# The third phase's mask added by a product on TensorE, and a head's three maxima by one VectorE reduction

## The chip, the cores and the metric

The kernel runs on one core of a Trainium2 chip. The metric is device time in microseconds, the median over several executions. One further execution was recorded by the profiler, and all rows below come from that one.

## The reference

A two-layer decoder on a batch of 8 samples, 256 tokens, width 128: a linear attention (phase 0), a cross attention of 16 heads over 512 context tokens with a key mask (phase 1), a mixture of eight experts, a windowed causal attention of 16 heads (phase 2), a differential cross attention of 8 heads with a feed-forward network, and a last feed-forward network with ternary weights. The change touches phase 2 alone:

```python
def _L1_attn_ref(x, w_in, b_in, w_out, b_out):        # B=8, s=256, E=128
    B, S, E, H, W = (4, 256, 128, 16, 128)
    HD = E // H                                       # 8
    ...
    scores = jnp.einsum('bhqd,bhkd->bhqk', q, k) / jnp.sqrt(jnp.asarray(HD, x.dtype))
    i = jnp.arange(s)[:, None]
    j = jnp.arange(s)[None, :]
    allowed = (j <= i) & (j >= i - W)                 # causal, window of 128
    scores = jnp.where(allowed[None, None], scores, jnp.asarray(-1000000000.0, x.dtype))
    attn = jax.nn.softmax(scores, axis=-1)
```

The softmax needs, for each query and head, a maximum over the allowed keys.

## The kernel before, in words

Each of the 8 samples goes through five chains of steps (`to0` to `to3`, `end`), on three lanes, and through four attention cores, one for each phase. A core has two parts. In the **maxima** part, TensorE multiplies queries with keys, with the queries on the partitions, into one of two PSUM banks `mb`; VectorE takes each row's maximum into `mx`. After a group of four heads, GpSimd (POOL) splits the negated maxima into three bf16 parts `nm` (L798 to L802), TensorE turns them (L973), VectorE copies them to `mrow` (L1446), and a DMA puts them as extra rows beside the queries in `QP`. In the **exponentials** part, TensorE computes the scores again with the keys on the partitions and the maximum already subtracted, adding the mask by a product with the identity `identb` (L1012 in phase 1, L1007 in phase 2), into two banks `eb`; ScalarE takes the exponential (L1183), and TensorE multiplies with the values (L1042). A planner at the top of the file writes one fixed order for each engine from a table of estimated durations. TensorE's order interleaves the maxima of one core with the exponentials of another and with the chains' steps, and so does VectorE's. Each engine works strictly through its own order, so an instruction that waits holds all behind it.

A unit of maxima in phase 2 is one head. There are 8 samples x 16 heads = 128 units, in 32 groups of four. The unit waits until VectorE has finished with the unit two before (`max_used`, since `mb` has two banks). Then TensorE multiplies the first 128 queries with the first 128 keys (L981, 128 columns), and the second 128 queries with all 256 keys (L982, 256 columns). VectorE adds the mask and takes the maximum in one instruction for each product (L1454 and L1455): the custom instruction `tensor_tensor_reduce` adds `winq_add` (0 or -1e30 for three blocks of 128 x 128), writes the sum to `junk` and the maximum to `mx`. In the trace each of these is a CUSTOM_DVE_ANT_0 row and a DVE_READ_ACCUMULATOR2_ANT row. The second one increments `max_used`, which frees the bank for TensorE and, at a group's fourth unit, lets POOL begin on `nm`. Phase 1's units add their mask in the same way (L1451); phase 3's have no mask and use a plain `tensor_reduce` (L1459).

Of the kernel before, what the change touches and what calls it, by code (L numbers as in the profile page):

```python
# [11 lines left out]
ALU = mybir.AluOpType  # L12
ACT = mybir.ActivationFunctionType
AX = mybir.AxisListType

P = 128
B, S, D, SK = 8, 256, 128, 512
TQ, TK = S // P, SK // P
# [10 lines left out]
NEG_EXP = -3.0e38  # L29
# [10 lines left out]
MAX_UNITS = (0, 8, 4, 8)  # L40
# [10 lines left out]
LANES, SLOTS, WIDES, OUTS, OB, QN, MROWS = 3, 3, 2, 3, 1, 3, 4  # L51
# [330 lines left out]
def decoder(nc, x, ctxT, maskq, maskk, weights, columns, rows_in, experts_bias, out):  # L382
    with ExitStack() as ctx:
        def sb(name, shape, dt=F32):
            return ctx.enter_context(nc.sbuf_tensor(name, shape, dt))
# [10 lines left out]
        def sbs(n, name, shape, dt=F32):  # L396
            return [sb(f"{name}{i}", shape, dt) for i in range(n)]
# [6 lines left out]
        identb = sb("identb", [P, P], BF16)  # L404
# [5 lines left out]
        winq_add = sb("winq_add", [P, 3, P], BF16)  # L410
# [14 lines left out]
        V = sbs(SLOTS, "V", [P, TK, 16, VW])  # L425
        KV = sbs(SLOTS, "KV", [P, 16, VW])
        qf = sbs(SLOTS, "qf", [P, P])
        mx = sbs(SLOTS, "mx", [P, TQ, 16])
        nmr = sbs(SLOTS, "nmr", [P, TQ, 16])
        nm = sbs(SLOTS, "nm", [P, TQ, 16, PARTS], BF16)  # L430
        mrow = sbs(MROWS, "mrow", [MAX_ROWS, S], BF16)
# [22 lines left out]
        junk = sb("junk", [P, 2, SK], BF16)  # L454
# [54 lines left out]
        def q_of(core, h, n=1):  # L509
            return QW[core.wide][0:WIDE_ROWS, h:h + n] if core.p == 3 else QP[core.slot][:, h:h + n]  # L510

        def k_of(core, h, lo, n):
            return KS[core.slot][0:WIDE_ROWS, h, lo:lo + n] if core.p == 3 else KS[core.slot][:, h // 2, lo:lo + n]
# [4 lines left out]
        def wait_alone(eng):  # L518
            eng.nop(nofuse=True)
# [7 lines left out]
        class Chain:  # L527
# [5 lines left out]
            def done(self, ins):  # L533
                self.n += 1
                ins.then_inc(self.sem, 1)
# [4 lines left out]
            def link(self, ins, plain=False):  # L540
                self.done(ins)
                self.wait()
                if plain:
                    wait_alone(self.eng)
# [116 lines left out]
        def _(pool):  # L661
            chain = Chain(pool, pool_step)
            link, done = chain.link, chain.done
# [125 lines left out]
            def max_event(e):  # L789

                if e.kind != "max" or e.i != MAX_UNITS[e.core.p] - 1:
                    return
                slot, g = e.core.slot, e.g
                pool.wait_ge(max_used, e.n + 3)
                m = mx[slot][:, :, 4 * g:4 * g + 4]
                r = nmr[slot][:, :, 4 * g:4 * g + 4]
                n = [nm[slot][:, :, 4 * g:4 * g + 4, a] for a in range(PARTS)]
                done(G.tensor_scalar(n[0], m, -1.0, None, ALU.mult))  # L798
                link(G.tensor_scalar(r, m, -1.0, None, ALU.mult))
                link(G.tensor_tensor(r, r, n[0], ALU.subtract))  # L800
                link(G.tensor_copy(n[1], r))
                G.tensor_tensor(n[2], r, n[1], ALU.subtract).then_inc(nm_ready, 1)  # L802

            def values():

                for i in range(SLOTS):
                    yield 0.5 + 5 * i
                    link(G.memset(V[i][:], 0.0))
                    G.memset(V[i][:, :, :, 16:17], 1.0).then_inc(values_init, 1)

            program(max_event, nothing, chain_steps, values())

        @block.tensor
        def _(pe):
# [150 lines left out]
            def max_event(e):  # L965
                core, g, i = e.core, e.g, e.i
                pe.wait_ge(max_used, e.n + 1)
                bank = mb[:, e.n % 2, :]
                if e.kind == "turn":
                    pe.wait_ge(nm_ready, NM_N[core.p, core.b, g] + 1)  # L970
                    dst = bank.bitcast(BF16)
                    for t in range(TQ):
                        ins = nc.tensor.transpose(dst[0:MAX_ROWS, t * P:(t + 1) * P],  # L973
                                                  nm[core.slot][:, t, 4 * g:4 * g + 4, :].rearrange("p h c -> p (h c)"), identb[:])
                    ins.then_inc(max_scores, 1)
                    return
                if g == 0 and i == 0:
                    pe.wait_ge(stack_in[core.slot], IN_SLOT[core.p, core.b][2])
                if core.p == 2:
                    h = 4 * g + i  # L980
                    nc.tensor.matmul(bank[:, 0:P], q_of(core, h)[:, 0, 0:P], k_of(core, h, 0, P), start=True, stop=True)  # L981
                    ins = nc.tensor.matmul(bank[:, P:3 * P], q_of(core, h)[:, 0, P:2 * P], k_of(core, h, 0, S), start=True, stop=True)  # L982
                else:
                    h, t = 4 * g + i // 2, i % 2
                    ins = nc.tensor.matmul(bank, q_of(core, h)[:, 0, t * P:(t + 1) * P], k_of(core, h, 0, SK), start=True, stop=True)  # L985
                ins.then_inc(max_scores, 1)
# [73 lines left out]
            def prelude():  # L1060
# [4 lines left out]
                pe.wait_ge(masks_ready, 1)  # L1065

            program(max_event, exp_event, chain_steps, prelude())

        @block.scalar
# [134 lines left out]
        def _(dve):  # L1204
            chain = Chain(dve, dve_step)
            link, done = chain.link, chain.done
            V_ = nc.vector
# [229 lines left out]
            def max_event(e):  # L1437
                core, g, i = e.core, e.g, e.i
                slot = core.slot
                bank = mb[:, e.n % 2, :]  # L1440
                dve.wait_ge(max_scores, e.n + 1)
                if e.kind == "turn":
                    n = TURN_N[core.p, core.b, g]
                    if n >= MROWS:
                        dve.wait_ge(mrow_in[n % MROWS], MROW_TO[n - MROWS])
                    V_.tensor_copy(mrow[n % MROWS][:], bank.bitcast(BF16)[0:MAX_ROWS, 0:S]).then_inc(max_used, 1)  # L1446
                    return
                wait_alone(dve)
                if core.p == 1:
                    h, t = 4 * g + i // 2, i % 2  # L1450
                    ins = V_.tensor_tensor_reduce(junk[:, e.n % 2, :], bank, maskq_add[:, t, :], 1.0, NEG_EXP, ALU.add, ALU.max, mx[slot][:, t, h:h + 1])  # L1451
                elif core.p == 2:
                    h = 4 * g + i
                    V_.tensor_tensor_reduce(junk[:, e.n % 2, 0:P], bank[:, 0:P], winq_add[:, 0, :], 1.0, NEG_EXP, ALU.add, ALU.max, mx[slot][:, 0, h:h + 1])  # L1454
                    ins = V_.tensor_tensor_reduce(junk[:, e.n % 2, P:3 * P], bank[:, P:3 * P], winq_add[:, 1:3, :].rearrange("p a k -> p (a k)"), 1.0, NEG_EXP,  # L1455
                                                  ALU.add, ALU.max, mx[slot][:, 1, h:h + 1])
                else:
                    h, t = 4 * g + i // 2, i % 2
                    ins = V_.tensor_reduce(mx[slot][:, t, h:h + 1], bank, AX.X, ALU.max)  # L1459
                ins.then_inc(max_used, 1)  # L1460

            def exp_event(e):
# [4 lines left out]
                if u >= PROBS:  # L1467
                    dve.wait_ge(av_done, u - PROBS + 1)
                V_.tensor_tensor(probs[:, u % PROBS, :].rearrange("p (j q) -> p j q", j=4), eb[:, u % 2, :].rearrange("p (j q) -> p j q", j=4),  # L1469
                                 tri[:].unsqueeze(1).to_broadcast([P, 4, P]), ALU.mult).then_inc(probs_by[0], 1)  # L1470

            program(max_event, exp_event, chain_steps, prelude())


# [66 lines left out]
```

## Time and profile before

| | us |
|---|---|
| median of 3 executions | 1154.66 |
| lowest and highest | 1147.33, 1155.74 |
| the profiled execution, its own time | 1146.01 |
| its span in the trace | 1144.3 |
| mean granted TensorE clock over it | 0.906 of 2.4 GHz |

The span is from the first instruction's start to the last one's end. TensorE (PE) is busy in 75% of it, VectorE (DVE) in 58%, ScalarE (ACT) in 40%, GpSimd (POOL) in 33%. PEld is TensorE's weight load, which runs beside its products. "The chain of waits" follows the work that ended last back to its beginning, at each step to what released it; "issue" in it is time for which the profile shows no wait. Ends of TensorE's rows are modelled and overlap; the distance from one start to the next is what a row holds the engine for.

### The profile page before, as it was taken

To read this page: it belongs to the slowest core of one execution; us is meant where nothing else is said; L and a number is where in the kernel's file an instruction comes from. 1 tells how busy PE (TensorE), PEld (TensorE's weight loads), DVE (VectorE), ACT (ScalarE), POOL (GpSimd) and SP (SyncE) were. 2 spreads that over 40 slices of the span, in tenths; PEclk is the share of its full clock that TensorE was granted. 3 is DMA by queue.
4 is the path that set the end of the run, shared out by engine and by line. 5 is a ranking of instruction groups with operands and counts; after the bars stand their busy time and mean duration, and the time that the engine had idled before them with its cause. 6 is when DMAs were issued, how large, how long until landed. Compare 5 with 4: busy or idle time off the path is not lost.

```text
span 1144.3 us, 19524 instructions
## 1 busy us (share of the span) xinstructions
PE 854.7 (75%) x6459; PEld 481.8 (42%) x6522; DVE 667.8 (58%) x2234; ACT 459.3 (40%) x923; POOL 383.1 (33%) x872
## 2 busy tenths in 40 slices
PE   0466757988888887887787677888988777874666
PEld 0244544334333343444443455553534434651345
DVE  6646655667776764765677474376566484444431
ACT  0322213554444443544454222654645334651432
POOL 7524343210313222443223246433232125360033
PEclk9778978999999998999999888899999698995877
DMA  5357774031220204641233334543120602224100
GB/s 177 101 88 165 166 168 90 11 56 32 42 49 16 51 19 86 125 96 53 57 56 81 59 78 108 138 73 58 35 53 16 104 2 53 64 64 76 16 1 10
DMA packets 124964, 79.84 MB, mean 70 GB/s; under 512 B 8312, under 2 KB 122176, under 8 KB 124736
## 3 DMA queue, kind: packets, MB, share of 16 engines
q1 hardware_dynamic: 124864, 78.59, 33.2%
q8 instruction: 52, 0.85, 0.3%
q14 instruction: 48, 0.39, 0.1%
HBM read 43.99 MB, written 32.90 MB: 67 GB/s over the span
## 4 chain that ended last, share of the span: by engine, by line
PE 42%; DVE 21%; issue 10%; POOL 10%; DMA 8%; SPq 4%; ACT 4%; another core or an unknown queue 1%; DVEq 0%; POOLq 0%; ACTq 0%
PE ob L1042 7%; PE mb L985 5%; POOL hn L707 4%; DMA KS<-bounce 4%; DVE junk L1451 3%; PE side L861 3%; PE eb L1012 3%; PE eb L1013 2%; DVE mx L1459 2%; DMA QW<-bounce 2%; PE side L916 2%; DVE An L1391 2%; PE side L899 2%; PE side L908 2%; POOL rstd L695 2%
## 5 line engine op out<-in xcount | busy, mean ns | idle before, releaser
L1183 ACT ACTIVATE probs<-eb 128x512 f32<-128x512 f32 (+1 forms) x512 | 287.5, 571 | 401.9 <-PE eb L1013 172.7
L1451 DVE CUSTOM_DVE_ANT_0 junk<-mb,maskq_add 128x512 bf16<-128x512 f32 x256 | 172.1, 690 | 110.1 <-PE mb L985 82.3
L798 POOL TENSOR_SCALAR nm<-mx 128x8 bf16<-128x8 f32 x80 | 20.7, 259 | 428.7 <-DVE mx L1451 193.4
L1042 PE MATMUL ob<-probs,V 128*32 128x256 f32 (+1 forms) x2048 | 138.3, 390 | 3.3 <-ACT probs L1183 2.1
L1459 DVE TENSOR_REDUCE mx<-mb 128x1 f32<-128x512 f32 x128 | 85.0, 687 | 75.8 <-PE mb L985 74.0
L1012 PE MATMUL eb<-maskk_add,identb 128*128 128x512 bf16 x256 | 99.9, 390 | 6.6 <-DMA QP<-mrow 2.7
L985 PE MATMUL mb<-KS,QP 128*128 128x512 bf16 x230 | 89.0, 394 | 13.0 <-DVE mx L1451 12.1
L1013 PE MATMUL eb<-QP,KS 128*128 128x512 bf16 x233 | 90.6, 389 | 0.0
L1042 PEld LDWEIGHTS ob<-probs,V 128*32 128x32 f32 x2048 | 55.4, 113 | 77.7 <-issue 46.3
L985 PE MATMUL mb<-KS,QW 112*128 112x512 bf16 x128 | 53.0, 432 | 36.0 <-DMA QW<-bounce 21.3
L1454 DVE CUSTOM_DVE_ANT_0 junk<-mb,winq_add 128x128 bf16<-128x128 f32 x128 | 37.1, 290 | 68.1 <-PE mb L982 66.4
L707 POOL TENSOR_SCALAR hn<-X,mv,rstd 128x128 f32<-128x128 f32 x80 | 72.2, 910 | 4.3
L821 PE MATMUL side<-ident,hn 128*128 128x128 f32 x80 | 18.8, 322 | 64.0 <-POOL hn L707 62.6
L1190 ACT COPY OT<-ob 128x512 f32<-128x512 f32 x56 | 32.7, 584 | 73.0 <-PE ob L1036 52.2
L1469 DVE TENSOR_TENSOR probs<-eb,tri 128x512 f32<-128x512 f32 x64 | 42.3, 685 | 32.8 <-PE eb L1002 31.4
L713 POOL TENSOR_TENSOR xs<-xs,scratch 128x256 f32<-128x256 f32 (+1 forms) x32 | 30.4, 950 | 92.5 <-ACT scratch L1118 57.0
L861 PE MATMUL side<-ident,OT 128*128 128x36 f32 (+1 forms) x448 | 55.7, 281 | 5.6 <-issue 5.3
L861 PEld LDWEIGHTS side<-ident,OT 128*128 128x128 f32 x448 | 55.6, 198 | 9.9 <-issue 8.3
L1016 PE MATMUL eb<-QW,KS 112*128 112x256 bf16 x256 | 50.3, 292 | 9.8 <-ACT probs L1183 3.4
L701 POOL TENSOR_SCALAR rstd<-mv 128x2 f32<-128x2 f32 x64 | 16.0, 250 | 120.1 <-DVE mv L1247 118.3
L985 PEld LDWEIGHTS mb<-KS,QP 128*128 128x128 bf16 x256 | 25.7, 101 | 68.4 <-DVE mx L1451 40.1
L1455 DVE CUSTOM_DVE_ANT_0 junk<-mb,winq_add 128x256 bf16<-128x256 f32 x128 | 53.8, 420 | 0.2 <-issue 0.2
(186 smaller groups left out, 1706.0 us busy)
## 6 DMA issues: line engine op xcount, KB each, us to landing
QP<-bounce SPq DMA_DIRECT2D x48, 256.0 KB, 5.6
KS<-bounce SPq DMA_DIRECT2D x32, 384.0 KB, 7.5
bounce<-scratch SPq DMA_DIRECT2D x48, 192.0 KB, 2.3
bounce<-scratch SPq DMA_DIRECT2D x64, 128.0 KB, 2.1
KS<-bounce SPq DMA_DIRECT2D x32, 192.0 KB, 5.9
bounce<-scratch SPq DMA_DIRECT2D x16, 384.0 KB, 2.6
cT<-ctxT_dram SPq DMA_DIRECT2D x16, 256.0 KB, 2.9
bounce<-scratch SPq DMA_DIRECT2D x16, 256.0 KB, 3.0
```

The lines of the kernel that those rows point to most:

```text
L707: ins = G.tensor_scalar(dst[:, t, :], src[:, t, :], mv[l][:, t, 0:1], rstd[l][:, t:t + 1], ALU.subtract, ALU.mult)
L861: ins = nc.tensor.matmul(bank[:, lo:lo + 4 * n].rearrange("p (h e) -> p h e", e=n), OT[o][:, g, t * P:(t + 1) * P], chosen, start=True, st ...
L985: ins = nc.tensor.matmul(bank, q_of(core, h)[:, 0, t * P:(t + 1) * P], k_of(core, h, 0, SK), start=True, stop=True)
L1012: nc.tensor.matmul(part, identb[:], maskk_add[:, kt:kt + 1, :].to_broadcast([P, 2, S]), start=True, stop=False, skip_group_check=True)
L1013: ins = nc.tensor.matmul(part, k_of(core, h, kt * P, P), q_of(core, h, 2), start=False, stop=True, skip_group_check=True)
L1016: ins = nc.tensor.matmul(bank[:, j * S:(j + 1) * S], k_of(core, h + j, kt * P, P), q_of(core, h + j)[:, 0, :], start=True, stop=True)
L1042: ins = nc.tensor.matmul(bank[32 * j:32 * j + 32, S - n:S], v_of(core, kt, 4 * g + j), pr[:, (j % 2) * n:(j % 2 + 1) * n], start=(kt == 0) ...
L1183: nc.scalar.activation(probs[:, u % PROBS, 0:n], eb[:, u % 2, 0:n], ACT.Exp, scale=SCALE[core.p]).then_inc(probs_by[1], 1)
L1451: ins = V_.tensor_tensor_reduce(junk[:, e.n % 2, :], bank, maskq_add[:, t, :], 1.0, NEG_EXP, ALU.add, ALU.max, mx[slot][:, t, h:h + 1])
L1455: ins = V_.tensor_tensor_reduce(junk[:, e.n % 2, P:3 * P], bank[:, P:3 * P], winq_add[:, 1:3, :].rearrange("p a k -> p (a k)"), 1.0, NEG_E ...
L1459: ins = V_.tensor_reduce(mx[slot][:, t, h:h + 1], bank, AX.X, ALU.max)
L1469: V_.tensor_tensor(probs[:, u % PROBS, :].rearrange("p (j q) -> p j q", j=4), eb[:, u % 2, :].rearrange("p (j q) -> p j q", j=4), tri[:].u ...
```

## The change

TensorE gets a third product in each phase-2 unit, ahead of the two. Identity times the three mask blocks, 384 columns of bf16, writes the mask into the bank, and the two score products then accumulate onto it. VectorE takes three maxima (one for each block of 128 keys) of the 384 sums by one plain `tensor_reduce`, into `mx[:, 0..2, h]`; `mx` gets a third row. After the fourth unit of a group, one small `tensor_tensor` takes the larger of rows 1 and 2 for the four heads at once, so that row 1 holds the second query tile's maximum as before. It waits for the reduction in front of it (`link`), and that fourth unit's `max_used` is now incremented by this small instruction. The order of the units and of all other instructions on every engine is the same.

```diff
-        mx = sbs(SLOTS, "mx", [P, TQ, 16])
+        mx = sbs(SLOTS, "mx", [P, 3, 16])
...
-                m = mx[slot][:, :, 4 * g:4 * g + 4]
+                m = mx[slot][:, 0:TQ, 4 * g:4 * g + 4]
...
                 if core.p == 2:
                     h = 4 * g + i
-                    nc.tensor.matmul(bank[:, 0:P], q_of(core, h)[:, 0, 0:P], k_of(core, h, 0, P), start=True, stop=True)
-                    ins = nc.tensor.matmul(bank[:, P:3 * P], q_of(core, h)[:, 0, P:2 * P], k_of(core, h, 0, S), start=True, stop=True)
+                    nc.tensor.matmul(bank[:, 0:3 * P], identb[:], winq_add[:].rearrange("p a k -> p (a k)"), start=True, stop=False, skip_group_check=True)
+                    nc.tensor.matmul(bank[:, 0:P], q_of(core, h)[:, 0, 0:P], k_of(core, h, 0, P), start=False, stop=True, skip_group_check=True)
+                    ins = nc.tensor.matmul(bank[:, P:3 * P], q_of(core, h)[:, 0, P:2 * P], k_of(core, h, 0, S), start=False, stop=True, skip_group_check=True)
...
                 elif core.p == 2:
                     h = 4 * g + i
-                    V_.tensor_tensor_reduce(junk[:, e.n % 2, 0:P], bank[:, 0:P], winq_add[:, 0, :], 1.0, NEG_EXP, ALU.add, ALU.max, mx[slot][:, 0, h:h + 1])
-                    ins = V_.tensor_tensor_reduce(junk[:, e.n % 2, P:3 * P], bank[:, P:3 * P], winq_add[:, 1:3, :].rearrange("p a k -> p (a k)"), 1.0, NEG_EXP,
-                                                  ALU.add, ALU.max, mx[slot][:, 1, h:h + 1])
+
+                    ins = V_.tensor_reduce(mx[slot][:, :, h:h + 1], bank[:, 0:3 * P].rearrange("p (a k) -> p a k", a=3), AX.X, ALU.max)
+                    if i == MAX_UNITS[2] - 1:
+                        link(ins)
+                        later = mx[slot][:, 1:3, 4 * g:4 * g + 4]
+                        ins = V_.tensor_tensor(later[:, 0, :], later[:, 0, :], later[:, 1, :], ALU.max)
```

## Rows read from the trace of the kernel before

**Rows 1.** The page: busy time by engine, and the chain of waits by engine.
```profile
PE 854.7 (75%) x6459; PEld 481.8 (42%) x6522; DVE 667.8 (58%) x2234; ACT 459.3 (40%) x923; POOL 383.1 (33%) x872
...
PE 42%; DVE 21%; issue 10%; POOL 10%; DMA 8%; SPq 4%; ACT 4%; another core or an unknown queue 1%; DVEq 0%; POOLq 0%; ACTq 0%
```

**Rows 2.** Busy time in the seven stretches that hold phase 2's maxima.
```profile
core 0: us, PE busy (x) PEld busy (x) DVE busy (x) ACT busy (x) POOL busy (x), PEclk, DMA share, GB/s
380.00:430.00 50.00, 40.41 (x306) 19.13 (x309) 33.92 (x184) 22.27 (x46) 15.56 (x53) 0.97 0.12 24
442.00:473.00 31.00, 23.37 (x192) 13.38 (x196) 17.49 (x97) 13.10 (x32) 14.31 (x32) 0.89 0.49 102
...
666.00:690.00 24.00, 20.18 (x159) 14.64 (x159) 16.60 (x83) 8.49 (x16) 10.96 (x32) 0.86 0.20 59
931.00:961.00 30.00, 20.80 (x179) 12.45 (x180) 20.39 (x105) 14.08 (x30) 15.88 (x43) 0.99 0.10 30
...
sum 204.00, PE 162.12 PEld 94.40 DVE 131.16 ACT 94.21 POOL 82.11; mean PE 23.16 PEld 13.49 DVE 18.74 ACT 13.46 POOL 11.73
```

**Rows 3.** Line 981, the wait before a unit's first product: total us, times.
```profile
  DVE mx L1455: 30.0, 55
```

**Rows 4.** The chain of waits, pieces at the unit's lines: start, us.
```profile
384.41 0.16 PE mb L981
1002.80 0.05 PE mb L981
...
1004.40 0.11 DVE junk L1454
```

**Rows 5.** The chain of waits by line, from 931 to 961 us, shares of it.
```profile
by line: issue 24.4%; POOL hn L707 10.6%; POOL rstd L695 9.6%; POOL rms L695 4.7%; POOL nm L798 3.4%; PE ob L1042 3.3%; DVE An L1391 3.3%; POOL rstd L701 3.1%; PE eb L1007 2.9%; POOL nm L802 2.9%; POOL nmr L800 2.9%; POOL nm L801 2.8%; POOL
```

**Rows 6.** TensorE's timeline, one place at full and one at half clock.
```profile
385.71 0.38 PE L1012 MATMUL eb<-maskk_add,identb 128*128 128x512 bf16 x1
385.93 0.38 PE L1013 MATMUL eb<-QP,KS 128*128 128x512 bf16 x1
...
416.34 0.63 PE L1012 MATMUL eb<-maskk_add,identb 128*128 128x512 bf16 x1
416.76 0.63 PE L1013 MATMUL eb<-QP,KS 128*128 128x512 bf16 x1
```

**Rows 7.** VectorE's timeline, a unit with the next one right behind it.
```profile
582.30 0.29 DVE L1454 CUSTOM_DVE_ANT_0 junk<-mb,winq_add 128x128 bf16<-128x128 f32 x1
582.52 0.42 DVE L1455 CUSTOM_DVE_ANT_0 junk<-mb,winq_add 128x256 bf16<-128x256 f32 x1
...
582.87 0.28 DVE L1454 CUSTOM_DVE_ANT_0 junk<-mb,winq_add 128x128 bf16<-128x128 f32 x1
```

**Rows 8.** VectorE's timeline, phase 3's plain reduction and linked small instructions.
```profile
587.29 0.29 DVE L1374 TENSOR_REDUCE rank<-xs 128x16 f32<-128x128 f32 x1
587.61 0.17 DVE L1375 SCALAR_TENSOR_TENSOR gate<-rank,gp 128x16 f32<-128x16 f32 x1
...
588.22 0.17 DVE L1378 TENSOR_TENSOR gate<-gate,grec 128x16 f32<-128x16 f32 x1
588.38 0.29 DVE L1454 CUSTOM_DVE_ANT_0 junk<-mb,winq_add 128x128 bf16<-128x128 f32 x1
...
594.34 0.69 DVE L1459 TENSOR_REDUCE mx<-mb 128x1 f32<-128x512 f32 x1 [0.41 <-PE mb L985]
594.95 0.27 DVE L1446 COPY mrow<-mb 12x256 bf16<-12x256 bf16 x1
```

**Rows 9.** Groups by line and shape: busy us, mean ns, idle before.
```profile
L1451 DVE CUSTOM_DVE_ANT_0 junk<-mb,maskq_add 128x512 bf16<-128x512 f32 x256 | 172.1, 690 | 110.1 <-PE mb L985 82.3 <-remote 24.3 <-DVE An L1391 0.9
L1459 DVE TENSOR_REDUCE mx<-mb 128x1 f32<-128x512 f32 x128 | 85.0, 687 | 75.8 <-PE mb L985 74.0
L1455 DVE CUSTOM_DVE_ANT_0 junk<-mb,winq_add 128x256 bf16<-128x256 f32 x128 | 53.8, 420 | 0.2 <-issue 0.2
L1454 DVE CUSTOM_DVE_ANT_0 junk<-mb,winq_add 128x128 bf16<-128x128 f32 x128 | 37.1, 290 | 68.1 <-PE mb L982 66.4 <-DVE An L1391 0.3 <-DVE hn L1335 0.3
```

## The prediction

> **What bounds the kernel now.** I read the page first: TensorE is busy in 75% of the span and holds 42% of the chain of waits, VectorE 58% and 21% [rows 1]. So no engine is full, and the end is set by a path that changes engines, most often TensorE's. The change touches only phase 2's maxima, so I looked next at the seven stretches that hold their 128 units, 204 us together [rows 2]. There TensorE's rows fill 162.12 us (79%) and VectorE's 131.16 us (64%). Both orders are fixed, so what a unit costs TensorE is not only its own affair: exponentials, experts and transposes queue behind it. The third view is the wait in front of a unit's first product: in 55 of 128 units TensorE waited there for VectorE to give the bank back, 30.0 us in all [rows 3]. In the other direction VectorE waited in front of L1454 for TensorE's L982, 66.4 us in all [rows 9], twice as long. In these units TensorE is the later one more often. The fourth view is the chain of waits itself: it runs through L981 in 60 of the 128 units and through L1454 in 44; of the 60 pieces the first and the last are shown, of the 44 the last [rows 4].
>
> **TensorE's part: one product and one weight load more for each unit.** A product holds the engine from its start to the next start. With 512 columns of bf16 that is 0.22 us at full clock and 0.42 us at half clock; three quarters of that is the mask product [rows 6]. So it takes 0.16 us at full clock, 0.32 us at half. The granted clock of the seven stretches, weighted by their lengths, is 0.95 (the four shown have 0.97, 0.89, 0.86 and 0.99 [rows 2]; the others 1.00, 0.92 and 1.00), so some 10% of the time is at half clock and the mean cost is 0.9 x 0.16 + 0.1 x 0.32 = 0.176 us. 128 of them are 22.5 us of TensorE. The added load of `identb` costs nothing of its own while a product streams before it, and the load of the queries goes under the mask product; where TensorE had to wait for the bank, the load of `identb` is bare, as that of the queries is now, so it replaces one. The mask product can't be started in the wait for the bank, since it writes to that bank. So the 55 waits hide nothing of it. What hides it is time in which TensorE would have waited later for something else. On the path I count the 60 units whose L981 is on the chain: 60 x 0.176 = **+10.6 us**. For the 68 others I take nothing, but they are the term that can only grow: all of them on a path would be 12 us more.
>
> **VectorE's part: two custom instructions become one reduction.** The rows' own durations mislead here. They are 290 and 420 ns, 0.71 us together [rows 9]; but a unit holds the engine for 582.30 to 582.87, that is 0.57 us, since the second starts 0.22 us after the first [rows 7]. A plain reduction of 512 elements lasts 0.69 us and holds the engine for 0.61 us (594.34 to 594.95) [rows 8]. From 290, 420 and 690 ns for 128, 256 and 512 elements, 128 elements are 0.13 us [rows 9]. So a reduction of 384 holds it for 0.48 us and lasts 0.56 us. That it has three results instead of one I cost at nothing: L1374 gives 16 results from 128 elements in 0.29 us, as long as the custom instruction takes for one [rows 8, 9]. Three of four units thus give 0.09 us back. The trace has no reduction of 384 from PSUM with three results; the nearest bounds are no gain (it holds the engine for 0.57 us, as now) and a gain of 0.15 us (by durations, 0.71 to 0.56). I take 0.09, from the start-to-start distances, since what waits behind is released by those.
>
> The fourth unit gets a small instruction behind a link. L1374 lasts 0.29 us and the linked L1375 starts 0.32 us after it, 0.03 us past its end; a small last one (L1378) holds the engine for 0.16 us [rows 8]. So this unit is 0.56 + 0.03 + 0.16 = 0.75 us, 0.18 more than now. In sum VectorE gets 96 x -0.09 + 32 x 0.18 = -8.6 + 5.8 = -2.8 us of occupation: nearly nothing. POOL's `nm` is released by this instruction and starts later by no more than that. On the chain are 44 units, 9 of them fourth ones by their place in the group: 35 x -0.09 + 9 x 0.18 = **-1.5 us**.
>
> A rule of the Trainium skill speaks against this part. VectorE: DVE Perf Modes, section Rules for kernel authors, says to expect 1x of `tensor_reduce`, calls it the slowest VectorE operation and advises restructuring away from it. The rows do not bear out the comparison here: 512 elements from PSUM take 687 ns reduced plainly and 690 ns with the mask added [rows 9]. If the plain one were slower per element, VectorE's term would turn positive; by the rows it is equal, and the sum keeps -1.5.
>
> **Sum.** +10.6 - 1.5 = +9.1 us. The profiled execution took 1146.0 us, so it would be 1155.1 us. The median shown, 1154.7 us, stands 8.7 us above it; with the same +9.1 us the forecast is **1164 us**, +0.8%. That the executions of one kernel already spread over 9.7 us (1146.0 to 1155.7) is why I count 1% (11.5 us) as the least that can be told from no change.
>
> **Rivals.**
> 1. *The product is on the path nearly everywhere.* Delaying the 68 other units lets new paths through TensorE form. For it: 79% filled, and the order is strict. Against it: in the 931 to 961 stretch TensorE is busy for 20.8 of 30 us and the chain lies mostly on POOL and in issue there [rows 2, 5]. It decides from some 75 units on. All 128: 22.5 - 1.5 = +21, **1176 us**. Chance 0.22.
> 2. *The clock gives it back.* In these stretches about a tenth of the time, 21 us, was granted half clock [rows 2]. If the added products keep the array busy enough to stay at full clock, work done in those 21 us with TensorE 79% filled would take half: up to 8 us back, and the sum is +1 to +2: **1156 us**. For it: the low clock stands in the rows of these stretches. Against it: four of the seven have 0.97 or more, where nothing is to be had, and the two lowest that are shown, 442 to 473 and 666 to 690, are low for reasons that the change leaves alone: TensorE's rows fill 75% and 84% of them already, so it isn't a want of products there. The Trainium skill (TensorE: Matmul & The Clock Gate, section The HAM clock gate) states the direction of it: the throttled state is the default and activity releases it. Chance 0.20.
> 3. *VectorE's order is the bound, and the change makes the kernel faster.* VectorE waits for TensorE now, but its chain in the stretches passes experts, splits and statistics as well. If those are released earlier, durations rather than distances count (0.71 to 0.56), and TensorE's waits for other engines swallow the product: 128 x -0.15 = -19.2, plus 32 small ones at 0.19, +6.1: -13 us, **1141.6 us**. It decides from the point where TensorE's product is off the path in nearly all units; 60 of 128 on the chain speak against it. Chance 0.07.
> 4. That the change doesn't do what it says: if the link or the third row made POOL wait longer, it would be a piece of rival 1; I give it no chance of its own.
>
> The forecast (+5 to +16 us around 1164, so 1159 to 1171) has the remaining 0.51. The range goes from rival 2 with some of the spread to rival 1: 1150 to 1178 us; what is left out is rival 3 and the extremes of 1. Below 1143.1 us (faster by over 1%) lies rival 3 alone: 0.06. Above 1166.2 us lie rival 1 and not quite 0.4 of the forecast's own case: 0.40. The rest, 0.54, is within 1%.
>
> **What would show it.** Right: TensorE with 128 more rows, each holding it for about 0.16 us; the plain reduction at 0.55 to 0.56 us, 0.48 to the next start; VectorE's wait in front of it longer than the 66.4 us now; L981's new line on the chain about 60 times or more. In the busy time TensorE should go up by more than 20 us while VectorE's falls by less than the durations say. Wrong: a stretch clock well off 0.95, which would move the sum by more than VectorE's part; a reduction held for over 0.57 us; or the mask product on the chain in fewer than 30 units, in which case TensorE had slack that I did not see.

## The result: 0.66% slower, and the profile after

| | before | after |
|---|---|---|
| median, us | 1151.86 (11 executions, 1147.33 to 1155.74) | 1159.34 (11, 1155.89 to 1163.45) |
| ratio to before | 1 | 1.0066, 95% interval 1.0047 to 1.0084 |
| profiled execution, us | 1146.01 | 1162.89 |

The change costs 7.6 us (5.4 to 9.7). The forecast was 1164 us, from a median of before that stood 2.8 us higher, or +9.1 us. The two profiled executions differ by more, 16.9 us, because that of before lies at the low end of its executions and that of after near the high end of its own; their mean granted clocks are 0.906 and 0.896. So the two traces serve to read single instructions and counts, and the ratio serves for the size.

The page of the changed kernel, the lines that answer to [rows 1]:

```profile
PE 884.7 (76%) x6584; PEld 500.2 (43%) x6650; DVE 664.1 (57%) x1882; ACT 460.3 (40%) x923; POOL 383.4 (33%) x872
...
PE 43%; DVE 18%; DMA 11%; POOL 9%; issue 9%; SPq 5%; ACT 3%; another core or an unknown queue 0%; DVEq 0%; POOLq 0%; ACTq 0%
```

TensorE's busy time rises by 30.0 us, more than the 22.5 us that the prediction counted for the products; this trace also had the lower clock. VectorE's falls by only 3.7 us although 352 of its rows are gone, near the 2.8 us that the prediction worked out from start-to-start distances; durations alone would have said 14.

The stretches with phase 2's maxima, in their new places, as in [rows 2]:

```profile
380.00:432.00 52.00, 44.95 (x334) 22.14 (x339) 32.58 (x95) 22.46 (x46) 15.47 (x53) 0.97 0.11 23
444.00:480.00 36.00, 28.56 (x204) 15.62 (x208) 16.82 (x53) 13.33 (x32) 14.76 (x34) 0.81 0.41 89
...
680.00:703.00 23.00, 20.64 (x172) 14.88 (x172) 15.52 (x38) 8.17 (x16) 11.24 (x31) 0.93 0.23 63
...
sum 214.00, PE 183.94 PEld 107.14 DVE 125.60 ACT 94.38 POOL 82.82; mean PE 26.28 PEld 15.31 DVE 17.94 ACT 13.48 POOL 11.83
```

The seven are 10 us longer together (214 us, though my borders are rounded). TensorE's rows now fill 86% of them instead of 79%. The granted clock (the third number from the end) did not rise over the seven: 0.97 stayed, 0.89 became 0.81, 0.86 became 0.93, and the mean weighted by length went from 0.95 to 0.93.

TensorE's timeline of the changed kernel, two units back to back at full clock. The first number is the start, the second the modelled duration:

```profile
385.43 0.33 PE L981 MATMUL mb<-winq_add,identb 128*128 128x384 bf16 x1
385.59 0.22 PE L982 MATMUL mb<-KS,QP 128*128 128x128 bf16 x1
385.65 0.27 PE L983 MATMUL mb<-KS,QP 128*128 128x256 bf16 x1
385.75 0.33 PE L981 MATMUL mb<-winq_add,identb 128*128 128x384 bf16 x1
385.92 0.22 PE L982 MATMUL mb<-KS,QP 128*128 128x128 bf16 x1
```

The mask product (now L981) holds TensorE for 0.16 to 0.17 us, from 385.43 to 385.59 and from 385.75 to 385.92. The whole unit takes 0.32 us of TensorE, half of it for the mask.

VectorE's timeline, to be read against [rows 7, 8]:

```profile
385.05 0.56 DVE L1456 TENSOR_REDUCE mx<-mb 128x3 f32<-128x384 f32 x1 [1.47 <-PE mb L983]
385.52 1.50 DVE L1392 SCALAR_TENSOR_TENSOR An<-side,gate,An 128x128 f32<-128x128 f32 x4
387.15 0.56 DVE L1456 TENSOR_REDUCE mx<-mb 128x3 f32<-128x384 f32 x1
387.75 0.16 DVE L1460 TENSOR_TENSOR mx<-mx 128x4 f32<-128x4 f32 x1
387.83 0.56 DVE L1456 TENSOR_REDUCE mx<-mb 128x3 f32<-128x384 f32 x1
```

A reduction lasts 0.56 us, and the next instruction starts 0.47 us after it. A fourth unit, with the link and the small instruction, takes from 387.15 to 387.83, that is 0.68 us, 0.21 more than the others (the prediction had 0.75 and 0.27; the small instruction is followed by the next one after 0.08 us, not 0.16).

The waits at the unit's two ends. First the group of the page (busy, mean | idle before it), then what TensorE waited for before the mask product (us, times), last who waited for the small instruction:

```profile
L1456 DVE TENSOR_REDUCE mx<-mb 128x3 f32<-128x384 f32 x128 | 70.2, 556 | 82.8 <-PE mb L983 81.6
...
  DVE mx L1456: 14.2, 34
...
  DVE mx L1460: 5.6, 6
...
  POOL nm L798: 106.7, 27
```

VectorE's wait in front of a unit grew from 66.4 us [rows 9] to 81.6 us. TensorE's wait for the bank before the unit's first product fell from 30.0 us in 55 units [rows 3] to 19.8 us in 40: 14.2 us in 34 for the reduction, and 5.6 us in 6 for the small instruction, which frees the bank at a group's end. Where TensorE was the later one of the two it now is so more often. The chain of waits runs through the mask product in 73 of 128 units (60 ran through the first product before) and spends 18.4 us there. It runs through the small instruction in 8 of 32 groups, for 1.3 us. Its share in the first stretch stands in the second place of this row of the chain by line, 380 to 432 us:

```profile
by line: PE ob L1043 11.0%; PE mb L981 8.9%; issue 7.5%; PE side L899 7.5%; DVE mx L1456 6.5%; PE eb L1013 6.5%; PE eb L1014 5.4%; DVE An L1392 4.5%; PE mb L983 4.5%; POOL hn L707 3.1%; PE mb L973 2.5%; PE mb L982 2.2%; PE eb L1008 2.1%; PE
```

### The profile page after: what moved, and what is told of

It reads as the page before. It is cut to its first block, busy times and chain, and to the rows that moved or that the text cites. A ratio compares the mean times of both kernels' runs of the same rounds, so it can differ in the third digit from the quotient of the medians.

```text
span 1161.2 us, 19425 instructions
## 1 busy us (share of the span) xinstructions
PE 884.7 (76%) x6584; PEld 500.2 (43%) x6650; DVE 664.1 (57%) x1882; ACT 460.3 (40%) x923; POOL 383.4 (33%) x872
## 4 chain that ended last, share of the span: by engine, by line
PE 43%; DVE 18%; DMA 11%; POOL 9%; issue 9%; SPq 5%; ACT 3%; another core or an unknown queue 0%; DVEq 0%; POOLq 0%; ACTq 0%
PE ob L1043 7%; DMA KS<-bounce 6%; PE mb L986 5%; POOL hn L707 3%; DMA QW<-bounce 3%; DVE junk L1452 3%; PE side L861 3%; PE eb L1013 3%; PE side L916 2%; PE eb L1014 2%; PE side L899 2%; DVE mx L1463 2%; DVE An L1392 2%; PE side L908 2%; PE mb L981 2%
## 5 line engine op out<-in xcount | busy, mean ns | idle before, releaser
L1456 DVE TENSOR_REDUCE mx<-mb 128x3 f32<-128x384 f32 x128 | 70.2, 556 | 82.8 <-PE mb L983 81.6
L986 PE MATMUL mb<-KS,QP 128*128 128x512 bf16 x230 | 90.4, 400 | 13.3 <-DVE mx L1452 12.4
L981 PE MATMUL mb<-winq_add,identb 128*128 128x384 bf16 x128 | 44.3, 346 | 22.0 <-DMA KS<-bounce 13.4
```

The costliest lines, as they stand in the source:

```text
L981: nc.tensor.matmul(bank[:, 0:3 * P], identb[:], winq_add[:].rearrange("p a k -> p (a k)"), start=True, stop=False, skip_group_check=True)
L1456: ins = V_.tensor_reduce(mx[slot][:, :, h:h + 1], bank[:, 0:3 * P].rearrange("p (a k) -> p a k", a=3), AX.X, ALU.max)
```

## Experiments

My theory: the product costs TensorE some 0.17 us in each unit and the path pays for about half of the units; VectorE's own gain is small, because the rows' durations overlap. The rivals were that the path pays for the product everywhere and VectorE gives much back, that TensorE has slack, and that the fourth unit's link is the real cost. All kernels were timed in five rounds against the kernel before; "us" is the ratio's excess times the median of before in that comparison (1149.5 to 1151.9 us). The numbers are given first as measured; the granted clock differs a little from kernel to kernel, and what that does to the readings stands behind the last experiment.

### e1, the product alone

```diff
 (to the kernel before, on TensorE only)
+ nc.tensor.matmul(bank[:, 0:3 * P], identb[:], winq_add[:].rearrange("p a k -> p (a k)"), start=True, stop=False, ...)
  (the two score products with start=False)
```

> The mask product is added on TensorE, and VectorE keeps its two custom instructions, which add the mask a second time (a masked key gets -2e30 instead of -1e30). It shows TensorE's term alone. Theory (the path runs through TensorE in about half of the units): +9 to +12 us against the kernel before, that is about 1162 us, 1 to 3 us above the kernel with the whole change. Rival 1 (the product is on the path nearly everywhere and VectorE gives back much): +18 to +22 us. Rival 3 (TensorE has slack): +0 to +4 us.

Measured: ratio 1.0108 (1.0070 to 1.0146), **+12.4 us** (8.0 to 16.8). Just above the +9 to +12 that the theory gave, and well below rival 1's value. In its trace the chain runs through the mask product in 72 units for 18.3 us, and VectorE's wait for TensorE is 78.6 us:

```profile
L1455 DVE CUSTOM_DVE_ANT_0 junk<-mb,winq_add 128x128 bf16<-128x128 f32 x128 | 37.1, 290 | 81.4 <-PE mb L983 78.6 <-DVE hn L1336 0.3 <-DVE An L1392 0.3
```

So that wait grows from 66.4 us by the product alone, whatever VectorE then does.

### e2, the reduction alone

```diff
 (to the change, on TensorE only)
- nc.tensor.matmul(bank[:, 0:3 * P], identb[:], winq_add[:]..., start=True, stop=False, ...)
  (the two score products with start=True again)
```

> The change without the mask product: the maxima are taken over all keys, the masked ones too, by the plain reduction and the fourth unit's small instruction. The mask is left out of the maxima only; the exponentials still have it. It shows VectorE's term alone. Theory: -1 to -3 us against the kernel before, about 1150 us. Rival 3 (durations count): -10 to -15 us. Rival (the link and the small instruction in the fourth unit cost more than the reduction gives): +1 to +5 us.

Measured: ratio 0.9981 (0.9962 to 1.0001), **-2.2 us** (-4.4 to +0.1), the theory's value. Rival 3 (-10 to -15 us) falls, and so does the rival that the link costs more than the reductions give (+1 to +5 us). The two halves add up to +10.2 us against the change's +7.6, within their intervals.

### e3, the product twice

```diff
+ (the mask product once more in front of itself, each with start=True)
```

> The whole change with the mask product issued twice (the second one starts the bank anew, so the sums are the same). It shows what a further 0.17 us of TensorE in each of 128 units costs. Theory (fixed share of the units on the path): +9 to +13 us against the change, about 1170 us. If the paths through TensorE fill up with what is added (the 68 others), +15 to +22 us. If the clock gives it back, +0 to +5 us, with a granted clock above that of the change.

Measured: ratio 1.0201 (1.0174 to 1.0228), **+23.1 us** (20.0 to 26.2), so +15 us over the change. 128 x 0.17 us are 22 us: the path pays for about two thirds of the second product, where it paid for about half of the first. The chain goes through the two products in 90 units. The clock does not give it back: the six executions have a mean of 0.900, as the change's eleven.

### e4 and e11, one maximum for both query tiles, no link

```diff
 (to the change)
- ins = V_.tensor_reduce(mx[slot][:, :, h:h + 1], bank[:, 0:3 * P].rearrange("p (a k) -> p a k", a=3), AX.X, ALU.max)
- if i == MAX_UNITS[2] - 1:
-     link(ins)
-     ... ins = V_.tensor_tensor(later[:, 0, :], later[:, 0, :], later[:, 1, :], ALU.max)
+ ins = V_.tensor_reduce(mx[slot][:, 0, h:h + 1], bank[:, 0:3 * P], AX.X, ALU.max)
 (POOL, phase 2)
+ m = mx[slot][:, 0:1, 4 * g:4 * g + 4].to_broadcast([P, TQ, 4])
```

> The whole change without the link and the small instruction: one reduction of all 384 sums into one maximum, used for both query tiles of the head (a bound for both, which the softmax allows), so the mask product stays and the fourth unit costs as much as the others. It shows what the fourth unit's link costs. Theory: 32 units get 0.27 us back, 9 of 44 on the path, so -2 to -3 us against the change, about 1157 us. Rival (POOL's start in each group is on the path): -6 to -9 us, which would undo the slowdown. Rival (the link is off the path): 0.

> e4_one_maximum again, beside e9_held_vectore on the same chip. If its gain over the change was real, +0 to +2 us against the kernel before; if chance, +5 to +8 us.

Measured: e4 1.0004 (0.9976 to 1.0032), **+0.5 us**; e11 0.9998 (0.9977 to 1.0019), **-0.2 us**. Against the change that is 7 to 8 us back, nearly three times what I had counted for the link. One result instead of three changes nothing in the reduction itself:

```profile
L1458 DVE TENSOR_REDUCE mx<-mb 128x1 f32<-128x384 f32 x128 | 69.7, 554 | 81.5 <-PE mb L985 80.0
```

554 ns against the change's 556, and VectorE's wait for TensorE remains, 80.0 us. What went is the fourth units' extra 0.21 us, 6.7 us in 32 groups. The time that came back is all of that and a little more, while the chain of the changed kernel had run through the small instruction in 8 of 32 groups only. So something else differs too: the mean granted clock of these executions is 0.906 (e4) and 0.908 (e11), that of before 0.902 in both comparisons.

### e6, the link alone

```diff
 (to the kernel before, behind the fourth unit's L1455)
+ link(ins)
+ later = mx[slot][:, 1, 4 * g:4 * g + 4]
+ ins = V_.tensor_tensor(later, later, later, ALU.max)
```

> The kernel before with a link and a small instruction (the maximum of row 1 with itself) behind the fourth unit's custom instructions, and nothing else changed. It shows the link's cost alone. Link theory (it delays POOL's start and the bank in each group): +5 to +8 us. Prediction's count: about +2 us (a quarter of 32 x 0.25 us). Off the path: 0.

Measured: ratio 1.0029 (1.0010 to 1.0048), **+3.3 us** (1.2 to 5.5). VectorE's timeline of this kernel shows what it adds to a fourth unit, which begins at 387.43:

```profile
387.99 0.09 DVE L1455 DVE_READ_ACCUMULATOR2_ANT mx<- 128x1 f32 x1
388.11 0.16 DVE L1460 TENSOR_TENSOR mx<-mx 128x4 f32<-128x4 f32 x1
388.23 0.29 DVE L1454 CUSTOM_DVE_ANT_0 junk<-mb,winq_add 128x128 bf16<-128x128 f32 x1
```

It is 0.80 us long instead of 0.57, so 7.4 us in 32 groups, of which the time pays 3.3. It lies between my count (about +2) and the link theory (+5 to +8).

### e7, the bank freed by the reduction

```diff
 (to the change, in the fourth unit: the reduction increments max_used)
+ dve.wait_ge(max_used, e.n + 3)
+ V_.tensor_tensor(later[:, 0, :], later[:, 0, :], later[:, 1, :], ALU.max).then_inc(two_ready, 1)
 (POOL waits for two_ready in phase 2)
```

> The whole change, but the fourth unit's reduction itself frees the bank, and the small instruction signals POOL alone by a semaphore of its own. Same work on each engine. If the late release of the bank is what the link costs, it gives back most of the 7 us that e4_one_maximum gave: -4 to -7 us against the change. If it is POOL's later start or VectorE's held order, 0 to -1 us.

Measured: ratio 1.0066 (1.0042 to 1.0091), **+7.6 us**; the change itself in the same comparison 1.0074 (1.0052 to 1.0095), +8.5 us (e8). The -4 to -7 us that an early release of the bank would have given did not come; the bank's later release is not the cost. That leaves POOL's start, VectorE's held order, or the clock.

> The change once more, on the same chip as the others of this set, so that they can be compared with it. Nothing is to be told apart: +5 to +10 us against the kernel before, as measured (1.0066).

### e9, VectorE held, nobody else late

```diff
 (to e4, in each fourth unit, behind the reduction that frees the bank and starts POOL;
  `spare` is a scratch tile, set once at the start)
+ dve.wait_ge(max_used, e.n + 3)
+ V_.tensor_tensor(spare[:, 0:4], spare[:, 4:8], spare[:, 4:8], ALU.max)
```

> e4_one_maximum (mask product, one reduction per unit, no small instruction that anybody waits for), and in each fourth unit VectorE waits for its own reduction and runs a small instruction on a scratch tile, as long as the link holds it in the change. Bank and POOL are released by the reduction. If the link's cost is VectorE's held order, it gives back the 7 us that e4_one_maximum won: +6 to +8 us against the kernel before. If the cost is POOL's later start, it stays at e4's +0 to +1 us. In between: both.

Measured: ratio 1.0030 (1.0010 to 1.0050), **+3.4 us** (1.1 to 5.7), where e11 on the same chip had -0.2. VectorE's timeline shows the same hold as in the change, 0.67 us from one reduction to the next:

```profile
384.52 0.56 DVE L1460 TENSOR_REDUCE mx<-mb 128x1 f32<-128x384 f32 x1
385.11 0.16 DVE L1467 TENSOR_TENSOR spare<-spare 128x4 f32<-128x4 f32 x1
385.19 0.56 DVE L1460 TENSOR_REDUCE mx<-mb 128x1 f32<-128x384 f32 x1
```

As measured, that puts about half of the link's 7 to 8 us on VectorE's held order, and the rest on POOL, which starts on `nm` later in the change (the second and third maximum take no time in the rows). But the executions of e9 have a mean clock of 0.904 and those of e11 0.908, and the chain of e9 runs through the small instruction in 2 of 32 groups. The split is therefore not shown.

### e10, a mask product of 128 columns

```diff
- nc.tensor.matmul(bank[:, 0:3 * P], identb[:], winq_add[:].rearrange("p a k -> p (a k)"), start=True, stop=False, ...)
+ nc.tensor.matmul(bank[:, 0:P], identb[:], winq_add[:, 0, :], start=True, stop=False, ...)
  (the second score product, on the other 256 columns, with start=True again)
```

> The change with a mask product of 128 columns instead of 384: only the first query tile gets its mask in the maxima, the second tile's is left out of them. The reduction and the link stay. If the product's cost goes with its columns, it is a third: e2_reduction_only (-2.2 us) + 12.4 / 3 = +2 us against the kernel before, about 1152 us. If it is an instruction's fixed cost (dispatch, the weight load), it stays near the change's +8 us.

Measured: ratio 0.9985 (0.9962 to 1.0008), **-1.7 us** (-4.4 to +0.9), against e2's -2.2 without any product. A fixed price for each instruction, which would have left it near +8 us, is excluded. But a third of the product's cost would have given about +2, and that lies just outside the interval too: less was measured than the columns say. Here too the mean clock was the higher one, 0.906. In the trace the product holds TensorE for 0.06 us, and the chain runs through this product in 59 units for 7.5 us, against 18.4 us for the one of 384 columns.

### e5 and e12, no product, one maximum

```diff
 (e4 without the mask product: the maxima run over masked keys too)
```

> No mask product, no small instruction: one plain reduction of the 384 unmasked sums into one maximum for both query tiles. The mask is left out of the maxima only. If the fourth unit's link really costs 7 us, as the difference of e4_one_maximum to the change suggests, this is e2_reduction_only (-2.2 us) less 7: -9 us, about 1141 us, faster than both kernels. If the link costs what the prediction counted (2 to 3 us), -4 to -5 us, about 1145 us. If e4's gain was chance, -2 us.

> e5_one_max_no_product again, as it is the one version below both kernels: -4 to -9 us against the kernel before if it holds. Less the measured e11_one_maximum_again it gives the product's cost a second time, in a kernel without the link: +6 to +12 us.

Measured: e5 0.9941 (0.9916 to 0.9967), **-6.8 us** (-9.7 to -3.8); e12 0.9938 (0.9916 to 0.9960), **-7.1 us** (-9.7 to -4.6). This version is 0.6% faster than the kernel before, and faster than the change. The value lies between the -9 us that a link of 7 us would have given and the -4 to -5 us of the prediction's count. VectorE's wait for TensorE is back where it was, as the group row shows:

```profile
L1457 DVE TENSOR_REDUCE mx<-mb 128x1 f32<-128x384 f32 x128 | 69.2, 553 | 70.9 <-PE mb L984 68.8
```

e4 less e5 and e11 less e12 (the latter on one chip) give the product's cost twice more, as measured: +7.3 and +6.9 us. The softmax is the same for any bound on its scores, as long as the bound isn't so far above an allowed score that the exponential vanishes. With these inputs masked keys are drawn like the allowed ones. For inputs whose masked scores tower over the rest this version would lose its digits; that was not tried.

**All runs at one clock.** Over the executions of one kernel, those with the lower mean granted clock are the longer ones. Of the 33 of before that were timed beside e9 to e12, the nine with 0.899 or less average 1153.4 us (mean clock 0.898), the ten with 0.904 or more 1148.2 us (0.905). A line fitted through all 198 executions of this case whose clock is on record, with one slope and a level for each kernel, gives 7.5 us for 0.01. With this estimate each result can be moved to the clock that before had beside it:

| | as measured, us | mean clock, before's beside it | at before's clock, us |
|---|---|---|---|
| e1, the product alone | +12.4 | 0.900, 0.902 | +10.9 |
| e2, the reduction and the link | -2.2 | 0.899, 0.902 | -4.1 |
| e3, the product twice | +23.1 | 0.900, 0.902 | +21.9 |
| e4, one maximum | +0.5 | 0.906, 0.902 | +3.3 |
| e11, the same | -0.2 | 0.908, 0.902 | +4.7 |
| e5, no product, one maximum | -6.8 | 0.902, 0.903 | -7.6 |
| e12, the same | -7.1 | 0.901, 0.902 | -7.9 |
| e6, the link alone | +3.3 | 0.901, 0.903 | +2.2 |
| e7, the bank freed first | +7.6 | 0.902, 0.903 | +6.8 |
| e8, the change | +8.5 | 0.901, 0.903 | +7.0 |
| e9, VectorE held | +3.4 | 0.904, 0.902 | +4.9 |
| e10, 128 columns | -1.7 | 0.906, 0.902 | +1.2 |

The four readings of the product, 12.4, 10.7, 7.3 and 6.9 us as measured, become 10.9 (e1), 11.1 (e8 less e2), 10.9 (e4 less e5) and 12.6 (e11 less e12). The five of the link, 3.3 to 8.7 us as measured, become 2.2 (e6), 3.5 and 3.8 (e2 less e5 and less e12), and 3.7 and 2.3 (e8 less e4 and less e11). The reductions alone give -7.6 and -7.9. The product of 128 columns costs 5.3 us (e10 less e2), about half of the 11 or so for 384, and the intervals allow a third. e9 lies 0.2 us above e11 and 1.6 above e4.

The numbers agree better this way, and the parts add up: 11 - 7.7 + 3 = +6, where the change has +7. But it stays an argument. Each value still has the 2 to 4 us of its measured interval on either side. No run shows whether a low clock makes an execution long or whether both come from a third thing; nor why e4, e10 and e11 have the higher one. If taking the link out is itself what raises the clock, then the 4 to 6 us between the two ways of reading are the link's after all, on another path than VectorE's order.

## Why the prediction was right, point by point

**The product, +10.6 us: right.** Held time per product 0.16 to 0.17 us as worked out, and the path pays for about half of 22.5 us: +12.4 (e1), +9.8 to +10.7 (e2 to the change), +7.3 (e4 and e5) and +6.9 (e11 and e12) as measured, 11 to 13 us at one clock. Counting the units on the chain of before gave 60; there were 73 afterwards. The remark that this term can only grow is borne out by e3, where the second product cost 15 us, a third to a half more than the first.

**VectorE's part, -1.5 us: the right sign and nearly the size in sum (e2: -2.2, at one clock -4.1), but the reductions' term was too small.** The reductions without the link give -6.8 and -7.1 us (e5, e12; -7.6 and -7.9 at one clock), where the count over 44 units says 44 x -0.09 = -4.0. The instruction times were right (0.47 and 0.48 us), so the share of the units that the path pays for was not: I took 44 of 128 from one execution's chain, and the runs say nearer to two thirds (7 of 11.5 us). For the link, 9 units x 0.27 = +2.4 were counted. The runs give +3.3 (e6), +4.6 (e5 to e2) or 7 to 8 us (e4 and e11 to the change) as measured, but 2 to 4 us at one clock, which the count fits; the chain of after has the small instruction in 8 of 32 groups. So read as measured, two errors cancelled. Read at one clock, the link's term was right, the reductions gave nearly 4 us more than counted, and that fits a change that cost a little less than +9.1. The statement that POOL's later start is contained in the 0.18 us is neither shown nor refuted, since e9 and e11 differ in their clock too.

**What is luck.** The stated range, 1150 to 1178 us, reaches from below the median of before (1151.9) to over three times the effect above it, so that the time fell into it says little. The forecast's level stood 4.7 us too high, 2.8 of it from the three executions that gave the median. What supports the mechanism is the difference (+9.1 against +7.6, 5.4 to 9.7) and the runs of each term.

**The price of three results at nothing: right.** 556 ns with three (after), 554 with one (e4). The rule of the Trainium skill (VectorE: DVE Perf Modes, section Rules for kernel authors) that calls `tensor_reduce` the slowest VectorE operation did not bear on this replacement: 384 elements took 556 ns, on the line between the 420 and 690 ns that the custom instruction takes for 256 and 512 [rows 9].

**Rival 1, the product on the path nearly everywhere: fell** for the first product (+12.4, not +21), though e3 goes toward it. **Rival 2, the clock: fell.** The mean granted clocks of the changed kernel's eleven executions were 0.896 to 0.907, 0.9005 on average; those of the kernel before in the later comparisons 0.896 to 0.909, 0.902 on average. Nothing was given back, and the weighted mean of the seven stretches went from 0.95 to 0.93. **Rival 3, VectorE's order as the bound: fell** as a forecast of a gain, since the product stays on the path; but the part of it that said that VectorE's order is worth more than its wait suggests holds: 7 us lie there without the product and the link.

## What to carry to other kernels

Moving an addition from VectorE to TensorE as a product with the identity is paid in columns of the fuller engine; here 384 columns for 0.09 us of VectorE, a bad trade. Two VectorE instructions in a row held the engine here for less than their durations say (0.57 us for 0.71), so count start to start, and count a link and the small instruction behind it as a term of its own: here 32 of them took a third to a half of what 128 reductions gave. Before a difference of a few us between two kernels is put down to an instruction, compare the mean granted clocks of their executions: here e4 and e11 had 0.005 to 0.008 more than the change, which by the estimate goes with 4 to 6 us, more than the link's own term. Ask first whether the mask is needed at all: a softmax's maximum may be any bound, and leaving it out of the maxima, with one maximum for both query tiles, was the only version clearly faster than the kernel before, by 0.6%.

## What was not expected of the hardware

The granted clock was the surprise. Kernels that differ by one small instruction in 32 places, or by the width of one product, ran at mean clocks from 0.899 to 0.908, and the higher clock goes with the shorter time, 7.5 us for 0.01. As measured, a product of 128 columns in each of 128 units, with its weight load, cost 0.5 us (e10 against e2, -1.7 and -2.2), while a link and a 161 ns instruction in 32 places cost 3.3 to 8 us. At one clock these are 5.3 and 2 to 4 us, beside held times of 128 x 0.06 = 7.7 and 32 x 0.21 = 6.7 us. What sets the clock apart between these kernels was not traced and stays open.
